# Second scan, last six states: the product with C wholly on VectorE, GpSimd only gathers

## The reference

```
u, res = split(x @ W_in);  u = silu(u);  delta = softplus(u @ W_delta + b_delta)
Bm = u @ W_B;  Cm = u @ W_C;  A = -exp(A_log)          # 16 columns each
h[t]  = exp(delta[t] * A) * h[t-1] + delta[t] * B[t] * u[t]   # 256 channels x 16 states
y[t]  = sum over states of h[t] * C[t];   y = (y + u * D) * silu(res);   out = y @ W_out
```

## Time and profile before

| | us |
|---|---|
| median of 3 runs | 794.63 |
| the runs | 794.22, 801.12, 794.63 |
| profiled execution, its time | 793.37 |
| its span, first to last instruction | 791.4 |

### The profile page before, as it was taken

How to read it: one execution, slowest core, us unless ns; L and a number is a source line. 1 busy time by engine, 2 the same in 40 slices (tenths; PEclk the granted TensorE clock), 3 DMA queues, 4 the chain that set the end, 5 groups by cost and what they waited for, 6 DMA issues and landing times. The chain is left out here.

```text
span 791.4 us, 11476 instructions
## 1 busy us (share of the span) xinstructions
PE 670.9 (85%) x3430; PEld 466.2 (59%) x3431; DVE 546.3 (69%) x846; ACT 398.3 (50%) x810; POOL 232.8 (29%) x183
## 2 busy tenths in 40 slices
PE   3889999999989925879899999999599799994665
PEld 2666777777758913335565555555447698882224
DVE  6174444444331303299999999999688899897897
ACT  1255565655523512846855566556338566663220
POOL 0012122112200043001123122315018356667880
PEclk9589999999996965989999999999889899997977
DMA  8400000000335921033657677769723455541112
GB/s 292 142 3 11 11 11 7 10 7 7 106 122 158 347 59 27 11 94 104 152 151 168 172 183 197 179 160 215 186 62 107 126 166 173 163 120 36 41 37 59
DMA packets 59801, 86.71 MB, mean 110 GB/s; under 512 B 7505, under 2 KB 35922, under 8 KB 59762
## 3 DMA queue, kind: packets, MB, share of 16 engines
q1 hardware_dynamic: 41330, 57.89, 23.8%
q0 software_dynamic: 7680, 23.08, 13.5%
q10 hardware_dynamic: 10752, 5.24, 2.2%
HBM read 54.60 MB, written 14.81 MB: 88 GB/s over the span
## 5 line engine op out<-in xcount | busy, mean ns | idle before, releaser
L1546 DVE TENSOR_REDUCE nmax<-PS 128x1 f32<-128x128 f32 (+7 forms) x128 | 95.8, 749 | 90.6 <-PE PS L987 90.5
L1015 PE MATMUL PS<-ROOM 128*128 128x512 f32 (+3 forms) x384 | 142.9, 490 | 0.5 <-ACT ROOM L671 0.5
L678 ACT ACTIVATE ROOM<-PS,nmax 128x128 f32<-128x128 f32 (+7 forms) x128 | 95.6, 747 | 76.7 <-DVE nmax L1546 74.7
L671 ACT COPY ROOM<-PS 128x512 f32<-128x512 f32 (+1 forms) x192 | 85.7, 483 | 77.5 <-PE PS L999 77.3
L999 PE MATMUL PS<-CST,ROOM 128*128 128x128 f32 x576 | 85.6, 276 | 10.8 <-ACT ROOM L671 10.8
L552 POOL DMA_DIRECT2D ROOM<-ROOM x32 | 28.5, 891 | 216.5 <-DVE ROOM L1630 214.3
L999 PEld LDWEIGHTS PS<-CST,ROOM 128*128 128x128 f32 x576 | 64.1, 141 | 39.3 <-issue 28.1
L984 PE MATMUL PS<-LATER 128*128 128x512 f32 (+2 forms) x192 | 76.7, 509 | 8.6 <-ACT ROOM L678 6.2
L1015 PEld LDWEIGHTS PS<-ROOM 128*128 128x128 f32 x384 | 65.1, 192 | 28.6 <-issue 25.3
L1622 DVE TENSOR_TENSOR_SCAN ROOM<-ROOM 128x1024 f32<-128x1024 f32 x32 | 72.7, 2271 | 0.5 <-ACT ROOM L710 0.2
L517 POOL DMA_INDIRECT rows_in<-XN,slot x48 | 65.2, 1359 | 21.9 <-issue 13.3
(11 more groups left out here) (176 smaller groups left out, 1244.6 us busy)
## 6 DMA issues: line engine op xcount, KB each, us to landing
ROOM<-bc_rows SPq DMA_DIRECT2D x32, 512.0 KB, 4.1
ROOM<-ROOM POOLq DMA_DIRECT2D x32, 512.0 KB, 5.8
LATER<-in_w SPq DMA_DIRECT2D x48, 256.0 KB, 2.9
ROOM<-in_w SPq DMA_DIRECT2D x32, 321.0 KB, 3.8
rows_in<-zero SPq DMA_DIRECT2D x20, 256.0 KB, 3.1
LATER<-rows_in SPq DMA_DIRECT2D x24, 128.0 KB, 2.6
rows_out<-ROOM ACTq DMA_DIRECT2D x24, 128.0 KB, 1.9
ROOM<-rows_in SPq DMA_DIRECT2D x8, 256.0 KB, 4.1
```

Of the source, the lines that this page charges most:

```text
L671: nc.scalar.copy(dst, src).then_inc(s_ed, 1)
L678: nc.scalar.activation(PR[:, s, 0:nk], sc[:, 0:nk], ACT.Exp, bias=nmax[:, i % 4:i % 4 + 1], accum_out=rsum[:, i:i + 1]).then_inc(s_ex, 1)
L1015: r = mm(PS[:, 6, lo:BANK], V[:, j, :], PT[:, 4 * group + j, lo:BANK], start=j == 0, stop=True, skip_group_check=True)
L1546: nc.vector.tensor_reduce(nmax[:, i % 4:i % 4 + 1], sc[:, 0:(i + 1) * P], AX_X, ALU.max, negate=True).then_inc(s_nm, 1)
```

## The change

For states 10 to 15, VectorE does the product with C of half 1 over all 1024 positions. GpSimd has no `quarter` there, only the gathers; ScalarE has no `copy_c` there. TensorE's waits for quarters go from `late` and from `add_y`. VectorE's scan of half 1 in state 10 waits for the quarter of state 8, as before; from state 11 on it waits for none, nor does the product wait for a copy of C.

```diff
@@ gpsimd
-            def quarter(n, late=None):
+            def quarter(n):
 
                 pool.wait_ge(s_sn, 2 * n + 2)
-                if late is None:
-                    pool.wait_ge(s_ya, 2 * n)
-                else:
-                    pool.wait_ge(s_yp, late)
+                pool.wait_ge(s_ya, 2 * n)
                 pool.wait_ge(s_cc, n + 1 - SHARED)
@@ gpsimd, the loop over the last six states
                     gather(1 + q // 2, k, 4 * q + t, G1b[q // 2][:, 8 * (q % 2) + 4 * k + t, :], s_g1[q])
-                quarter(n, 2 * (n - LATE) if n > LATE else None)
@@ scalar
             decay(LATE, True)
-            copy_c(LATE)
             pair_out(2 * PAIRS - 1, 1, 16 * PAIRS - 16)
             with act.Fori(LATE + 1, STATE) as n:
                 decay(n, True)
-                copy_c(n)
@@ tensor, add_y
                 pe.wait_ge(s_hc, 2 * n + c + 1)
-                if c == 1:
-                    pe.wait_ge(s_hp, n + 1 - SHARED)
@@ tensor, late
                 spread_b(n + 1)
                 add_y(n, 0, n is LATE)
-                spread_c(n + 1)
+                spread_c(n + 1, True, False)
                 add_y(n, 1, n is LATE)
@@ vector, state
                         dve.wait_ge(s_hc, u + c - 1)
-                        if c == 1 and shared > 1:
+                        if c == 1 and (shared > 1 or n is LATE):
                             dve.wait_ge(s_hp, n - SHARED)
@@ vector
-            state(LATE, True)
+            state(LATE, True, shared=0)
             with dve.Fori(LATE + 1, STATE) as n:
-                state(n, True, late=True)
+                state(n, True, late=True, shared=0)
```

## The result

| | before | changed |
|---|---|---|
| median, us | 794.22 (5 runs) | 783.16 (5 runs) |
| the runs | 792.94 to 801.12 | 782.88 to 787.38 |
| profiled execution: time, span | 793.37, 791.4 | 787.38, 785.6 |
| start of state 10 on VectorE | 711.42 | 716.17 |
| from there to the first combination | 62.97 | 53.60 |

The ratio is 0.9854, with a 95% interval from 0.9818 to 0.989: 1.5% faster, 11.1 us by the medians.

A forecast was written before the change was run, and what follows sets the result against it. GpSimd's queue was taken as the bound, VectorE next: 9.3 us earlier at the first combination plus 0.6 in it, less 0.2 for hand-overs, gives 9.7 off 794.6, so 784.9 us; range 783.2 to 788.3.

The forecast's parts named there:

- (a): VectorE's half 1 product with C, 512 to 1024 columns in six states: 0.54 us per state, 3.24 us, unhidden.
- The pace, 8.90, and 9.3 us at the first combination: VectorE's states at 8.90 us each, so the combination after state 15 begins at 765.1, 9.3 us earlier.
- (b): Quarters leave GpSimd: 6.7 us idle before scans and 1.73 us of scan stretch go.
- (c): VectorE's 3.1 us of waits for TensorE go if it keeps up; added TensorE wait taken as 0.
- rival 2: TensorE at the low clock becomes the bound: 786.8 to 789 us, chance 9%.
- (e): GpSimd's 32 gathers in one row, five held 1.8 us each at most; last landed 768.8, 3 us of cover.
- (f): Whether the denser gathers hold VectorE's scans: between 0 and 0.94 us per scan, taken as 0.
- The other reading beside it: All-SBUF VectorE work and GpSimd's SBUF-reading instructions exclude each other, whoever came first; kept as rival, not in the sum.
- Rivals 1, 2 and 3: Gathers in flight hold scans, 10%; TensorE at low clock bounds, 9%; VectorE's free state is 8.56 us, 8%.
- rival 4: Held gathers become the end, ahead of the second combination; 805 us at 18 held, chance 3%.
- The 0.2 us for hand-overs: Taken off the 9.9 us gain because a VectorE instruction starting after a wait doesn't overlap the one before.
- "The tail stays": After the second combination: TensorE's output product of 6.13 us, VectorE's last addition and the store remain unchanged.

The follow-up runs named there:

- e1: Kernel before, with the 32 gathers put behind all six quarters in GpSimd's queue; 813.47 us, stage (state 10 to first combination) 50.46 us.
- e2: Kernel before, with each of the six quarters moved ahead of its state's six gathers; 784.62 us, ratio 0.9875.
- e3: Changed kernel, with the half 1 product with C left at 512 positions in the last six states; 776.45 us, ratio 0.9779.
- e9: Kernel before, quarters of states 10 to 14 behind four gathers each, state 15's ahead of the last 12; stage from state 10 to first combination 55.94 us.
- e4: Changed kernel with 8 more gathers ahead of the 32; from state 10 to first combination 53.60 us, tail 18.37 us.
- e7: Kernel before, with the change made in states 13 to 15 only; 788.13 us, ratio 0.9938.
- mix: Changed kernel, but GpSimd keeps the quarters of states 10 to 12, each ahead of four gathers, 20 gathers following in states 13 to 15; 784.87, then 780.90 us.
- e0: Changed kernel timed again, nothing altered; 784.20 us, ratio 0.9884.
- e6: Changed kernel with four spreads added on TensorE between its last addition and output product; stage 53.60 us, tail 15.77 us.

## Why the prediction was right or wrong

- **GpSimd's queue as the bound, and VectorE as the next.** Right; e1, e2 and e3 show it. The prediction had named the place behind six gathers, but moved the quarters away and didn't ask what their place alone was worth: 8.05 us of stage by order alone (e2), 12.51 with no gather ahead (e1), at no cost in width.
- **(a) Width, 0.54 per state.** 0.52 (e3).
- **The pace, 8.90, and 9.3 us at the first combination.** 8.88 and 9.37.
- **(b), the first combination 0.6 shorter.** 4.53, as put.
- **(c) TensorE.** 0 waits, as taken. The 3.1 us were listed as waits that go if TensorE keeps up; e1 and e9 show them as a consequence of the late quarter. But the price at the low clock was misread. The addition of 3.05 us stood at a granted clock of 0.64; wholly at 0.50 it takes 3.78, in the changed kernel:

```profile
724.36 3.78 PE L1253 MATMUL PS<-ROOM,CST 128*128 128x512 f32 x4
728.78 3.78 PE L1253 MATMUL PS<-ROOM,CST 128*128 128x512 f32 x8
```

  With it a state is some 2 x 0.85 + 2 x 3.57 = 8.8 us of TensorE (an estimate from starts in this trace), and 12.4 with a third addition. So the 1.8 us of room held against rival 2 weren't there. What kept it away is the other reason given: the clock rose. TensorE worked without a break from 723.34, was at 0.50 until 729 and at 1.00 from 730 on; the next two additions, begun at 728.78, took 3.78 together.
- **(e) Gathers.** Five held, at 1.0 to 1.4 us each and not 1.8. Cover 5.0 us to the start of the second combination, against 3 predicted. The prediction and the section on the kernel before take that start for the moment when all gathers are wanted; the last eight are wanted 2.3 us later, by the second half of the combination.
- **(f) Scans begun under a gather.** 0, as taken. The other reading beside it needs a word: the stretched scan at 756.27 began 0.59 us before its quarter (756.86), so it had come first and still ended late, 2.16 us after the quarter's end. Rivals 1, 2 and 3 did not occur, nor rival 4, which e4 shows to be 7.3 us of gathers away.
- **The 0.2 us for hand-overs.** Failed: VectorE had no wait left in states 11 to 15, so there was none to pay.
- **"The tail stays".** This is the term that was mis-sized. With 0.6 off for the combination it was put at 16.4 and measured 15.75 to 15.83. TensorE's output product took 5.47 instead of 6.13 us, at a granted clock of 0.69 against 0.61, and VectorE's wait before the last addition fell from 1.05 to 0.39: 0.66 us. I had read 6.13 as fixed, though the row is one at a low clock. What sets that clock stays open, and before has a single profile, so how much of the 0.66 comes of the change isn't shown.

Together 0.2 for hand-overs, 0.6 in the tail (16.44 put, 15.83 measured) and 0.05 of pace: 9.7 predicted, 10.55 measured from state 10 on. The other 0.9 of the 1.7 us between forecast and median is not the mechanism's: 0.4 is the median of before, which moved from 794.63 to 794.22 with two more runs, and 0.5 is scatter (11.06 by the medians, 10.55 by the stretches).

- **The range.** Its lower end, 783.2, was too close. It let the forecast's own case reach only 1.3 us down (783.6), with 0.4 us between two runs as their scatter, while 801.12 stood beside them. Against the 10.55 of the stage the medians gave 11.06, 9.3 and 11.6 us in three timings. The 95% intervals of these ratios reach 2.5 to 3.1 us to either side, and a range for this program needs as much for that alone. That the median missed the range by 0.04 us, and not by more or less, is chance; the 0.85 us missing from the sum are not.

## What to carry to other kernels

When an engine's queue holds both slow work that nobody waits for and short work that others wait for, put the short work first and see that a period of the queue, with its held instructions, stays below the period of the engine that waits. Only then ask whether the short work is worth moving. A late hand-over costs more than its own wait where a second engine has to make up for it (2.07 us late, 5.25 us lost).

## What the runs showed of the hardware

- A gather issued under an all-SBUF scan ends 0.7 to 0.8 us after the scan (issued 728.67, ended 730.65; the scan ended 729.90). A scan begun under a gather in flight isn't lengthened: the changed kernel's five took at most 2.293 us.
- GpSimd's tensor operation does stretch such a scan. In the last six states of all profiles, the five scans that met the end of a quarter ended 2.15 to 2.17 us after it, whether the quarter began first (3.16, 3.09 and 2.49 us in e2 and before, 2.55 in e7) or 0.59 us after the scan (4.02 in before). The other way round, a quarter behind a gather that was issued within 0.03 us of the scan's start took 2.40 to 2.42 us instead of 1.27 and ended 1.05 or 1.06 us after the scan, which took 2.34 or 2.35 (twice in before, once in e2 and in e7).
- TensorE's output product, 32 matmuls of the same shape, took 3.84, 5.46, 6.13 or 6.47 us, at granted clocks of 1.00 (mix, e4), 0.69 (changed, e0, e6), 0.61 (before) and 0.57 (e9). Neither the idle time ahead of it (5.46 after 2.42 and after 4.14, 3.84 after 2.48) nor the work before that orders them: behind additions of 5.40 us it took 5.47 in the changed kernel and 3.84 in the mix. What sets the clock there stays open.
